# A selective-scan layer with router: turned input products as diagonal products on TensorE, and the state sum in [channel, time]

## The chip, the cores and the metric

The kernel runs on one core of a Trainium2 chip. The metric is the device time of one execution in microseconds. The engines are PE (TensorE: matrix products and transposes), DVE (VectorE), ACT (ScalarE), POOL (GpSimd) and SP (SyncE, which issues the DMAs). In the profile a matrix instruction has two rows, PE for the stream and PEld for the loading of its stationary operand.

## The reference, cut to what matters

Two sequences of 2048 positions with 512 features go through a state-space layer and then a layer that weighs 64 expert biases. All is float32. The part that the change touches is the scan:

```python
delta = jax.nn.softplus(x @ W_delta_1 @ W_delta_2 + b_delta_2)     # [b, l, 1024]
Bm = x @ W_B; Cm = x @ W_C                                          # [b, l, 16]
def step(h, inp):                                                   # h: [b, e = 1024, n = 16]
    A_bar = jnp.exp(d_l[:, :, None] * A)
    h = h * A_bar + (d_l * x_l)[:, :, None] * B_l[:, None, :]
    y_l = jnp.einsum('ben,bn->be', h, C_l)
    return (h, y_l)
...
y_skip = (y + x * W_D) * _silu(skip)
return resid + y_skip @ W_out
```

For each channel e and state n the kernel needs u = (delta x)[e, l] B[l, n], the recurrence along l, and the sum over n of h[e, l] C[l, n].

## The kernel before, in words

The 4096 positions are cut into 16 chunks of 256. Every engine's program is written out by hand as a loop over steps, and within a step over 32 slots. In step t the scan works on chunk t - 3; two chunks form a stage of 512 positions, and a step scans a half of the 1024 channels over the whole stage, in two quarters (256 channels, held as two tiles `q` of 128). One slot is one state n of one quarter: 16 states times 2 quarters are 32 slots. Other jobs ride along in fixed slots: `norm` three chunks ahead, `prep` (in-projection, convolution, delta, B and C) two ahead, `gate` one behind, `mix` (skip product, gate, output product) two behind, `route` (router and experts) three behind. So steps 0 and 1 of the scan have no mix, the last two have no prep, and three steps stand before the scan and three behind it.

One slot runs like this. ACT makes the decay exp(delta A) (`decay`, L703), a 128x512 tile for each q. For 6 of the 16 states (`PLAIN_STATES`) the decay goes into the PSUM tile `bank[:, q]` and POOL makes u with a 128x1024 product into `operand` (`make_u`, L592), from a row of B that a DMA spread over all partitions. For the other 10 the decay goes into `operand`; u is made turned, in [time, channel], where B is a number per partition: ACT multiplies the turned dx (`dx_t`) by it (`make_ut`, L722), and PE turns it back, 4 transposes of 128x128 for each q, into `bank[:, q]` (`turn_u`, L1129). DVE then scans each q (L953) and copies the last column to `carry` (L924). POOL multiplies h by C (`weigh`, L608), and PE adds the result over the 16 states in the PSUM tile `y_sum`, which lies as [time, channel]: 8 transposing 128x128 instructions a slot that accumulate (`add_y`, `add_turned`, L1134), behind 8 products of x with diag(D) at the first state of a quarter (L1152).

There is one `bank` for each q: the transposes of slot s + 1 wait for the scan of slot s in the same q, and the scan of slot s + 1 waits for them. Each engine takes its instructions strictly in the order written. PE's order within slot s is: u of slot s + 1 for q = 0, half of the sum for slot s - 2, side work, u for q = 1, the other half of the sum, side work. DVE's is the two scans of slot s, then its side work: convolution (L1013), x (L993), expert sum o (L1103), and the gate (L1037) and its product (L1049).

`mix` reads the sum back from DRAM as `acc` in [time, channel], PE turns it into `mixed` (L1329), and DVE multiplies it with the gate into `ys`. The output product (L1339) then takes `ys` as its stationary operand.

```python
for b in range(SB):
    last = transpose(bank[:, q, b * P:(b + 1) * P], u_t[:, j % 2, b, q * P:(q + 1) * P], ident[:])
```

Of the kernel before, what the change touches and what calls it, by code (L numbers as in the profile page):

```python
# [23 lines left out]
N = 16  # L24
# [21 lines left out]
NORMED = 8  # L46

# [52 lines left out]
PLAIN_STATES = (0, 3, 5, 8, 11, 13)  # L100
TURNED_STATES = tuple(n for n in range(N) if n not in PLAIN_STATES)


def turned_u(n):

    return n in TURNED_STATES


def before(states, s):

    return s // N * len(states) + sum(n < s % N for n in states)


def build(nc, resid, norm_w, w_skip, w_in, conv_w, conv_b, w_delta_1, w_delta_2, b_delta_2, w_b, w_c, a_log,
# [13 lines left out]
    y_dram = nc.dram_tensor("y_dram", [2, 2, PAIRS, P, TB, QE], F32).ap()  # L128
# [5 lines left out]
    with ExitStack() as stack:  # L134
# [35 lines left out]
        y_out = sb("y_out", P, SB, QE)  # L170


        acc = sb("acc", P, 2, TB, QE)
        thg, gate = sb("thg", P, 2, 2, T), sb("gate", P, 2, 2, T)
# [13 lines left out]
        y_sum = stack.enter_context(nc.psum_tensor("y_sum", [P, SB, QE], F32))  # L188
# [14 lines left out]
        u_ready = signal("u_ready", "scan", before(PLAIN_STATES, SLOTS))  # L203
        ut_ready = signal("ut_ready", "scan", before(TURNED_STATES, SLOTS))
        ut_turned = signal("ut_turned", "scan", 2 * before(TURNED_STATES, SLOTS))
# [8 lines left out]
        b_loaded = [loads_of(f"b_loaded{k}", "scan", before(PLAIN_STATES, SLOTS) // 2) for k in range(2)]  # L214
# [25 lines left out]
        y_turned, ys_ready = signal("y_turned", "mix", PAIRS), signal("ys_ready", "mix", PAIRS)  # L240
# [105 lines left out]

        def prepared(t, half):

            return (FIRST + t) // 2 * 2 + half - 2 - FIRST
# [5 lines left out]
        with nc.Block() as block:  # L355
            @block.sync
            def _(sp):
                def load_quarter(t, k):
# [11 lines left out]
                    if v := due(sp, u_ready, t - 1, len(PLAIN_STATES) * (k + 1)):  # L370
                        sp.wait_ge(u_ready.sem, v)
# [15 lines left out]
                def load_b(t, s):  # L387
# [5 lines left out]
                    if turned_u(n):  # L393
                        return
                    j = before(PLAIN_STATES, s)
# [40 lines left out]
                def load_acc(t, p):  # L436
# [6 lines left out]
                    if v := due(sp, y_turned, t, p - 1):  # L443
                        sp.wait_ge(y_turned.sem, v)
                    sp.dma_start(acc[:, p % 2], y_dram[chunk // 2 % 2, chunk % 2, p]).then_inc(
                        acc_loaded[p % 2].sem, 16)

                def store_y(t, k):
# [9 lines left out]
                    sp.dma_start(y_dram[stage % 2, :, quarter].rearrange("h p b e -> p h b e"),  # L458
                                 y_out[:].rearrange("p (h b) e -> p h b e", h=2)).then_inc(y_stored.sem, 16)
# [101 lines left out]
            def _(pool):  # L561
# [15 lines left out]
                def make_u(t, s):  # L577
# [4 lines left out]
                    _, _, n, k, number = place(t, s)  # L582
                    if turned_u(n):
                        return
                    j = before(PLAIN_STATES, s)
# [96 lines left out]
            def _(act):  # L682
# [3 lines left out]
                def decay(t, s, q):  # L686
# [7 lines left out]
                    if turned_u(n):  # L694
# [11 lines left out]
                def make_ut(t, s, pair):  # L706
# [4 lines left out]
                    stage, _, n, k, _ = place(t, s)  # L711
                    if not turned_u(n):
                        return
                    j = before(TURNED_STATES, s)
                    if v := due(act, dxt_ready, t, 2 * k + pair + 1):
                        act.wait_ge(dxt_ready.sem, v)
                    if v := due(act, bt_ready, prepared(t, pair), 1):
                        act.wait_ge(bt_ready.sem, v)
                    if v := due(act, ut_turned, t, 2 * j - 2):
                        act.wait_ge(ut_turned.sem, v)  # L720
                    for b in (2 * pair, 2 * pair + 1):
                        last = nc.scalar.activation(u_t[:, j % 2, b], dx_t[:, k, b], ACT.Copy,  # L722
                                                    scale=b_t[:, stage % 2, b, n:n + 1])
                    if pair:
                        last.then_inc(ut_ready.sem, 1)

                def take_dxt(t, k, pair):
                    if not slot_of(t, 0):
                        return
                    if v := due(act, dxt_turned, t, 2 * k + pair + 1):  # L730
# [4 lines left out]
                def take_y(t, k):  # L735
# [6 lines left out]
                    for pair in range(2):  # L742
# [639 lines left out]
```

## Time and profile before

| what | value |
|---|---|
| device time, median of 3 runs | 2380.34 us (2379.85 to 2382.69) |
| the profiled execution's own time | 2379.91 us |
| its span in the profile | 2378.0 us |
| busy share: PE, DVE, ACT, POOL | 82%, 75%, 70%, 80% |
| mean granted TensorE clock | 0.939 of full |
| first scan, last scan start | 124.9 us, 2221.6 us |

The profiled execution has 1.9 us outside its span, and lies 0.4 us under the median. The span falls into a head of 124.9 us before the first scan, 16 steps of 32 slots up to the start of the last scan, and a tail of 156.4 us. Busy shares are unions of rows; a PE row is longer than the distance to the next one, since matrix instructions overlap. So what a PE instruction costs in a dense stretch is read from the distance between starts.

### The profile page before, as it was taken

Reading aid. Unit: us, or ns where it says so; the run is one execution under the profiler, and the core shown is the slowest. Engines: PE = TensorE matmul, PEld = TensorE weight load, DVE = VectorE, ACT = ScalarE, POOL = GpSimd, SP = SyncE. Lnnn points to the kernel's source line nnn. Section 1 sums busy time; section 2 is a strip of 40 time slices with the busy share of each in tenths; the row PEclk is TensorE's granted clock in tenths of the full one; section 3 lists DMA queues with packets and bytes.
Section 4 is the critical chain, followed back from the end, with each engine's and each line's share of the span. In section 5 each row is a group of like instructions: output and inputs, shape, how many; then the busy total and the mean of one; then the engine's idle time right before and its main releaser. Section 6 shows DMA issues by size and latency. Waiting matters only on the chain. (4 is left out here: it accounts for less than half of the span.)

```text
span 2378.0 us, 35550 instructions
## 1 busy us (share of the span) xinstructions
PE 1958.7 (82%) x11717; PEld 1584.2 (67%) x11717; DVE 1795.4 (75%) x3105; ACT 1669.1 (70%) x3276; POOL 1913.5 (80%) x1192
## 2 busy tenths in 40 slices
PE   5577777898889898898889898898889988797883
PEld 3456666777667676777667686776667776666551
DVE  3377877798697977888697977889697887887522
ACT  2368686877769685787779686786868687787421
POOL 1279898898789797989879897998879898999512
PEclk9988988999999999999999999999999999999996
DMA  4555556665747565674657556574757646555320
GB/s 159 169 178 182 189 177 215 201 216 157 225 151 239 180 215 183 203 229 150 210 175 235 196 186 215 185 228 148 232 169 222 194 154 207 181 183 160 120 71 18
DMA packets 239281, 434.31 MB, mean 183 GB/s; under 512 B 19134, under 2 KB 135418, under 8 KB 239098
## 3 DMA queue, kind: packets, MB, share of 16 engines
q1 hardware_dynamic: 239098, 432.04, 56.9%
q8 instruction: 94, 1.54, 0.3%
q14 instruction: 89, 0.73, 0.1%
HBM read 347.57 MB, written 84.41 MB: 182 GB/s over the span
## 5 line engine op out<-in xcount | busy, mean ns | idle before, releaser
L608 POOL TENSOR_TENSOR hc<-h,c_all 128x1024 f32<-128x1024 f32 x512 | 1205.0, 2365 | 219.5 <-DVE h L953 160.0
L953 DVE TENSOR_TENSOR_SCAN h<-operand,carry,bank 128x512 f32<-128x512 f32 x480 | 597.1, 1271 | 174.1 <-PE bank L1129 142.7
L1134 PE MATMUL y_sum<-ident,hc 128*128 128x128 f32 x4096 | 624.7, 281 | 13.0 <-POOL hc L608 12.7
L1129 PE MATMUL bank<-ident,u_t 128*128 128x128 f32 x2560 | 417.3, 288 | 243.2 <-DVE h L953 219.7
L722 ACT ACTIVATE u_t<-dx_t,b_t 128x256 f32<-128x256 f32 x1280 | 575.0, 499 | 0.5 <-PE bank L1129 0.5
L1129 PEld LDWEIGHTS bank<-ident,u_t 128*128 128x128 f32 x2560 | 312.4, 148 | 375.1 <-issue 240.2
L1134 PEld LDWEIGHTS y_sum<-ident,hc 128*128 128x128 f32 x4096 | 506.1, 146 | 79.8 <-issue 50.2
L592 POOL TENSOR_TENSOR operand<-dx_q,b_all 128x1024 f32<-128x1024 f32 x192 | 454.5, 2367 | 11.0 <-DMA b_all<-bc_dram 11.0
L703 ACT ACTIVATE bank<-delta_q,neg_a 128x512 f32<-128x512 f32 x384 | 262.5, 684 | 263.1 <-DVE h L953 262.7
L703 ACT ACTIVATE operand<-delta_q,neg_a 128x512 f32<-128x512 f32 x640 | 432.9, 714 | 0.0
L953 DVE TENSOR_TENSOR_SCAN h<-bank,carry,operand 128x512 f32<-128x512 f32 x288 | 354.9, 1270 | 33.1 <-POOL operand L592 16.4
L1339 PE MATMUL mixed<-wout,ys 128*128 128x512 f32 x512 | 272.8, 623 | 3.5 <-DVE ys L1049 3.5
L1259 PE MATMUL pair_bank<-rnt,win 128*128 128x256 f32 x1024 | 261.9, 404 | 11.1 <-DVE x L993 9.0
L1315 PE MATMUL routed<-rnt_gate,wskip 128*128 128x256 f32 x1024 | 245.2, 384 | 22.9 <-DVE gate L1037 18.9
L953 DVE TENSOR_TENSOR_SCAN h<-operand,bank 128x512 f32<-128x512 f32 x160 | 189.7, 1211 | 66.4 <-PE bank L1129 48.4
L1259 PEld LDWEIGHTS pair_bank<-rnt,win 128*128 128x128 f32 x1024 | 201.6, 205 | 57.1 <-issue 28.5
L1315 PEld LDWEIGHTS routed<-rnt_gate,wskip 128*128 128x128 f32 x1024 | 187.2, 191 | 54.6 <-issue 29.6
L1013 DVE SCALAR_TENSOR_TENSOR hv<-pair_bank,taps,hv 128x253 f32<-128x253 f32 (+2 forms) x384 | 181.5, 473 | 0.0
L953 DVE TENSOR_TENSOR_SCAN h<-bank,operand 128x512 f32<-128x512 f32 x96 | 112.8, 1210 | 46.9 <-ACT bank L703 36.5
L684 ACT ACTIVATE hv<-pair_bank,cbias,taps 128x253 f32<-128x253 f32 x128 | 64.9, 557 | 103.9 <-PE pair_bank L1259 103.9
L642 POOL TENSOR_TENSOR dx<-delta,x 128x1024 f32<-128x1024 f32 x32 | 75.6, 2365 | 34.5 <-ACT delta L815 34.5
L1339 PEld LDWEIGHTS mixed<-wout,ys 128*128 128x128 f32 x512 | 81.9, 197 | 29.1 <-issue 22.4
(124 smaller groups left out, 2009.3 us busy)
## 6 DMA issues: line engine op xcount, KB each, us to landing
c_all<-bc_dram SPq DMA_DIRECT2D x256, 512.0 KB, 4.3
b_all<-bc_dram SPq DMA_DIRECT2D x192, 256.0 KB, 5.2
win<-in_L_attn_W_in SPq DMA_DIRECT2D x64, 512.0 KB, 5.7
wskip<-in_L_attn_W_skip SPq DMA_DIRECT2D x64, 512.0 KB, 6.2
x_dram<-x SPq DMA_DIRECT2D x64, 256.0 KB, 4.5
delta_dram<-delta SPq DMA_DIRECT2D x32, 512.0 KB, 7.3
dx_dram<-dx SPq DMA_DIRECT2D x32, 512.0 KB, 7.3
delta_q<-delta_dram SPq DMA_DIRECT2D x32, 512.0 KB, 5.8
```

The costliest lines, as they stand in the source:

```text
L592: nc.gpsimd.tensor_tensor(operand[:, number % 3], dx_q[:, k], b_all[:, j % 2:j % 2 + 1].to_broadcast([P, 2, SPAN]), ALU.mult).then_inc(u_r ...
L608: nc.gpsimd.tensor_tensor(hc[:, number % 3], h[:, number % 3], c_all[:, j % 2, s % 2:s % 2 + 1].to_broadcast([P, 2, SPAN]), ALU.mult).then ...
L642: nc.gpsimd.tensor_tensor(dx[:, part], delta[:, part], x[:, part], ALU.mult).then_inc(dx_ready.sem, 1)
L703: nc.scalar.activation(to, delta_q[:, k, q], ACT.Exp, scale=neg_a[:, et, n:n + 1]).then_inc(exp_ready.sem, 1)
L722: last = nc.scalar.activation(u_t[:, j % 2, b], dx_t[:, k, b], ACT.Copy, scale=b_t[:, stage % 2, b, n:n + 1])
L953: nc.vector.tensor_tensor_scan(h[:, number % 3, q], first, second, start, ALU.mult, ALU.add).then_inc(scan_done.sem, 1)
L1013: return nc.vector.scalar_tensor_tensor(out=to, in0=of, scalar=taps[:, et, k:k + 1], in1=onto, op0=ALU.mult, op1=ALU.add)
L1129: last = transpose(bank[:, q, b * P:(b + 1) * P], u_t[:, j % 2, b, q * P:(q + 1) * P], ident[:])
L1134: return matmul(to, lhsT=of, rhs=ident[:], is_transpose=True, start=start, stop=stop, skip_group_check=True)
L1259: last = matmul(pair_bank(p)[:, e * T:(e + 1) * T], win[:, p % 2, k, e * P:(e + 1) * P], rnt[:, k, :], start=(k == 0), stop=(k == KD - 1))
L1315: last = matmul(routed[:, e * T:(e + 1) * T], wskip[:, p % 2, k, e * P:(e + 1) * P], rnt_gate[:, k, :], start=(k == 0), stop=(k == KD - 1))
L1339: last = matmul(mixed[:], ys[:, et, b * P:(b + 1) * P], wout[:, et, :], start=(et == 0), stop=(et == ET - 1))
```

## The change

It has five parts. (1) u of 24 slots in 32 instead of 20 is made on PE, and POOL keeps 8 instead of 12. (2) On PE those are no longer transposes of ACT's product, but products: the stationary operand is the turned dx, and the moving one is diag(B), a 128x128 tile for each block of 128 positions. ACT now makes diag(B) from the identity (128x128) instead of u (128x256), into a ring of 4. (3) `y_sum` lies as [channel, time]: h C is added by a product with the identity, one 128x512 instruction for each q. (4) `mix` therefore reads `acc` as it needs it; PE's turning of it is gone, the gate stays in the PSUM tile `routed`, and DVE multiplies that with `acc`. (5) The in-projection of the first channel pair of a chunk stands one slot earlier, and the second half of the output product one slot later.

```diff
-PLAIN_STATES = (0, 3, 5, 8, 11, 13)
+PLAIN_SLOTS = (0, 4, 7, 10, 16, 21, 27, 30)
...
-    y_dram = nc.dram_tensor("y_dram", [2, 2, PAIRS, P, TB, QE], F32).ap()
+    y_dram = nc.dram_tensor("y_dram", [2, PAIRS, P, 2, SPAN], F32).ap()
...
-        u_t = sb("u_t", P, 2, SB, QE)
+        diag_b = sb("diag_b", P, RING, SB, P)
...
-                def make_ut(t, s, pair):
+                def make_diag(t, s, pair):
...
-                    if v := due(act, ut_turned, t, 2 * j - 2):
-                        act.wait_ge(ut_turned.sem, v)
+                    if v := due(act, u_turned, t, 2 * (j - RING + 1)):
+                        act.wait_ge(u_turned.sem, v)
+                    ring = ring_of(t, j)
                     for b in (2 * pair, 2 * pair + 1):
-                        last = nc.scalar.activation(u_t[:, j % 2, b], dx_t[:, k, b], ACT.Copy,
+                        last = nc.scalar.activation(diag_b[:, ring, b], ident[:], ACT.Copy,
                                                     scale=b_t[:, stage % 2, b, n:n + 1])
...
                                         nc.vector.scalar_tensor_tensor(
-                                            out=gate[:, p % 2].rearrange("p e t -> p (e t)"),
-                                            in0=thg[:, p % 2].rearrange("p e t -> p (e t)"), scalar=1.0,
+                                            out=routed[:], in0=thg[:, p % 2].rearrange("p e t -> p (e t)"), scalar=1.0,
...
                                         nc.vector.tensor_tensor(
-                                            ys[:, 2 * p:2 * p + 2, :].rearrange("p e t -> p (e t)"), mixed[:],
-                                            gate[:, p % 2].rearrange("p e t -> p (e t)"),
+                                            ys[:, 2 * p:2 * p + 2, :].rearrange("p e t -> p (e t)"), routed[:],
+                                            acc[:, p % 2].rearrange("p e t -> p (e t)"),
                                             ALU.mult).then_inc(ys_ready.sem, 1)
...
                     for b in range(SB):
-                        last = transpose(bank[:, q, b * P:(b + 1) * P], u_t[:, j % 2, b, q * P:(q + 1) * P],
-                                         ident[:])
-                    last.then_inc(ut_turned.sem, 1)
+                        last = matmul(bank[:, q, b * P:(b + 1) * P], dx_t[:, k, b, q * P:(q + 1) * P],
+                                      diag_b[:, ring_of(t, j), b], start=True, stop=True)
+                    last.then_inc(u_turned.sem, 1)
...
-                        for b in (2 * pair, 2 * pair + 1):
-                            for q in range(2):
-                                last = matmul(y_sum[:, b, q * P:(q + 1) * P], lhsT=x_q[:, q, b * P:(b + 1) * P],
-                                              rhs=diag_d[:, 2 * quarter + q], start=b % 2 == 0 and q == 0,
-                                              stop=False, skip_group_check=True)
+                        last = matmul(y_sum[:, q], lhsT=diag_d[:, 2 * quarter + q], rhs=x_q[:, q], start=True,
+                                      stop=False)
...
-                    for b in (2 * pair, 2 * pair + 1):
-                        for q in range(2):
-                            last = add_turned(y_sum[:, b, q * P:(q + 1) * P], hc[:, number % 3, q, b * P:(b + 1) * P],
-                                              False, n == N - 1)
+                    last = matmul(y_sum[:, q], lhsT=ident[:], rhs=hc[:, number % 3, q], start=False, stop=n == N - 1)
...
-                                if (s, late) in ((3 * p - 2, 1), (3 * p - 1, 0)):
+                                first = 3 * p - 2 if p else -3
+                                if (s, late) in ((first, 1), (first + 1, 0)):
...
-                                if s == 3 * p + 15 and not late:
...
-                                            last = transpose(mixed[:, (2 * e + b) * P:(2 * e + b + 1) * P],
-                                                             acc[:, p % 2, b, e * P:(e + 1) * P], ident[:])
```

The first place is PE in the middle of a step that has a mix job, around slots 14 to 16: u into `bank`, the sum into `y_sum`, the skip product into `routed`. Before:

```order
L1129 MATMUL bank<-ident,u_t 128x128 x4
L1134 MATMUL y_sum<-ident,hc 128x128 x4
L1277 MATMUL pair_bank<-x,wbc 32x256 x4
L1315 MATMUL routed<-rnt_gate,wskip 128x256 x4
L1134 MATMUL y_sum<-ident,hc 128x128 x4
L1329 MATMUL mixed<-ident,acc 128x128 x4
L1134 MATMUL y_sum<-ident,hc 128x128 x4
```

The same place after the change:

```order
L1130 MATMUL bank<-diag_b,dx_t 128x128 x4
L1153 MATMUL y_sum<-hc,ident 128x512
L1269 MATMUL pair_bank<-x,wbc 32x256 x4
L1307 MATMUL routed<-rnt_gate,wskip 128x256 x4
L1153 MATMUL y_sum<-hc,ident 128x512 x2
```

Four transposing instructions of 128 columns have become one product of 512 columns, the four transposes into `bank` four products, and the turning of `acc` is gone.

The second place is PE at the end of a step, slots 29 to 31, with the first in-projection of the next chunk (`win`). Before:

```order
L1184 MATMUL pair_bank<-ident,dx_q 128x128 x4
L1129 MATMUL bank<-ident,u_t 128x128 x4
L1134 MATMUL y_sum<-ident,hc 128x128 x4
L1129 MATMUL bank<-ident,u_t 128x128 x4
L1134 MATMUL y_sum<-ident,hc 128x128 x4
L1259 MATMUL pair_bank<-rnt,win 128x256 x4
L1134 MATMUL y_sum<-ident,hc 128x128 x4
L1259 MATMUL pair_bank<-rnt,win 128x256 x4
```

After:

```order
L1175 MATMUL pair_bank<-ident,dx_q 128x128 x4
L1251 MATMUL pair_bank<-rnt,win 128x256 x4
L1130 MATMUL bank<-diag_b,dx_t 128x128 x4
L1153 MATMUL y_sum<-hc,ident 128x512
L1251 MATMUL pair_bank<-rnt,win 128x256 x4
L1130 MATMUL bank<-diag_b,dx_t 128x128 x4
L1153 MATMUL y_sum<-hc,ident 128x512 x3
```

The in-projection now stands right behind the turning of dx, and not behind the sum of the next slots.

## Rows read from the trace of the kernel before

**Rows 1.** The page: busy time, share of the span and instructions of each engine.

```profile
PE 1958.7 (82%) x11717; PEld 1584.2 (67%) x11717; DVE 1795.4 (75%) x3105; ACT 1669.1 (70%) x3276; POOL 1913.5 (80%) x1192
```

**Rows 2.** Stretches: head, scan span, tail, and two neighbouring full steps.

```profile
core 0: us, PE busy (x) PEld busy (x) DVE busy (x) ACT busy (x) POOL busy (x), PEclk, DMA share, GB/s
0.00:124.90 124.90, 71.66 (x274) 53.62 (x275) 41.87 (x133) 42.84 (x90) 22.29 (x46) 0.90 0.53 175
124.90:2221.60 2096.70, 1784.86 (x11055) 1466.42 (x11055) 1710.31 (x2860) 1594.95 (x3127) 1855.87 (x1086) 0.95 0.60 192
2221.60:2378.00 156.40, 102.13 (x392) 64.15 (x390) 43.20 (x113) 31.31 (x60) 35.32 (x61) 0.84 0.18 61
...
1452.90:1584.90 132.00, 117.16 (x734) 95.62 (x733) 112.64 (x194) 103.89 (x205) 117.35 (x74) 0.97 0.63 201
1584.90:1726.00 141.10, 120.41 (x734) 97.44 (x733) 112.65 (x194) 104.07 (x205) 121.67 (x76) 0.95 0.62 193
```

**Rows 3.** Groups by line and form on PE, whole span.

```profile
L1134 PE MATMUL y_sum<-ident,hc 128*128 128x128 f32 x4096 | 624.7, 281 | 13.0 <-POOL hc L608 12.7
...
L1129 PE MATMUL bank<-ident,u_t 128*128 128x128 f32 x2560 | 417.3, 288 | 243.2 <-DVE h L953 219.7 <-ACT u_t L722 19.4
...
L1339 PE MATMUL mixed<-wout,ys 128*128 128x512 f32 x512 | 272.8, 623 | 3.5 <-DVE ys L1049 3.5
...
L1152 PE MATMUL y_sum<-diag_d,x_q 128*128 128x128 f32 x512 | 67.7, 275 | 0.7 <-ACT y_out L744 0.7
...
L1152 PEld LDWEIGHTS y_sum<-diag_d,x_q 128*128 128x128 f32 x512 | 65.8, 192 | 4.4 <-issue 2.1
```

**Rows 4.** PE's timeline in slots 0 to 2: start, time, line.

```profile
1460.62 0.60 PE L1134 MATMUL y_sum<-ident,hc 128*128 128x128 f32 x4
1461.06 1.02 PE L1339 MATMUL mixed<-wout,ys 128*128 128x512 f32 x2
1461.92 0.60 PE L1134 MATMUL y_sum<-ident,hc 128*128 128x128 f32 x4
...
1464.58 1.89 PE L1259 MATMUL pair_bank<-rnt,win 128*128 128x256 f32 x8
1466.31 1.05 PE L1152 MATMUL y_sum<-diag_d,x_q 128*128 128x128 f32 x8
1467.19 0.60 PE L1134 MATMUL y_sum<-ident,hc 128*128 128x128 f32 x4
```

**Rows 5.** Waits on PE and DVE, 1183.4 to 1726 us (four steps): total, times, longest.

```profile
PE bank L1129 <- DVE h L953: 48.3, 30, 5.2
PE pair_bank L1184 <- DMA dx_q<-dx_dram: 12.0, 2, 6.3
...
DVE h L953 <- PE bank L1129: 48.0, 33, 9.2
```

**Rows 6.** DVE's timeline behind the scans of slots 3 and 6.

```profile
1471.23 0.13 DVE L924 TENSOR_REDUCE carry<-h 128x2 f32<-128x2 f32 x1
1471.28 0.68 DVE L993 SCALAR_TENSOR_TENSOR x<-pair_bank,hv 128x512 f32<-128x512 f32 x1
...
1473.94 2.44 DVE L953 TENSOR_TENSOR_SCAN h<-operand,carry,bank 128x512 f32<-128x512 f32 x2
...
1484.68 0.13 DVE L924 TENSOR_REDUCE carry<-h 128x2 f32<-128x2 f32 x1
...
1488.05 2.44 DVE L953 TENSOR_TENSOR_SCAN h<-operand,carry,bank 128x512 f32<-128x512 f32 x2
```

**Rows 7.** Groups on ACT and POOL that the change touches, whole span.

```profile
L722 ACT ACTIVATE u_t<-dx_t,b_t 128x256 f32<-128x256 f32 x1280 | 575.0, 499 | 0.5 <-PE bank L1129 0.5
...
L592 POOL TENSOR_TENSOR operand<-dx_q,b_all 128x1024 f32<-128x1024 f32 x192 | 454.5, 2367 | 11.0 <-DMA b_all<-bc_dram 11.0
...
L748 ACT ACTIVATE diag_d<-ident,dskip 128x128 f32<-128x128 f32 x8 | 2.4, 387 | 0.7 <-PEq L322 0.7
```

More of the change, by code:

```diff
@@ L46 @@
 NORMED = 8
+RING = 4
 class Signal:
@@ L97, in jobs_of, with turned_u, before @@
     return tuple(job for job, chunk in ahead.items() if 0 <= chunk < CHUNKS)
-PLAIN_STATES = (0, 3, 5, 8, 11, 13)
[L101 to L111, printed above, removed]
+PLAIN_SLOTS = (0, 4, 7, 10, 16, 21, 27, 30)
+TURNED_SLOTS = tuple(s for s in range(SLOTS) if s not in PLAIN_SLOTS)
+def turned_u(s):
+    return s in TURNED_SLOTS
+def before(slots, s):
+    return s // SLOTS * len(slots) + sum(n < s % SLOTS for n in slots)
 def build(nc, resid, norm_w, w_skip, w_in, conv_w, conv_b, w_delta_1, w_delta_2, b_delta_2, w_b, w_c, a_log,
@@ L213, in build @@
         xq_loaded, y_stored = loads_of("xq_loaded", "scan", 2), loads_of("y_stored", "scan", 2)
-        b_loaded = [loads_of(f"b_loaded{k}", "scan", before(PLAIN_STATES, SLOTS) // 2) for k in range(2)]
+        b_loaded = [loads_of(f"b_loaded{k}", "scan", before(PLAIN_SLOTS, SLOTS) // 2) for k in range(2)]
         c_loaded = [loads_of(f"c_loaded{k}", "scan", SLOTS // 4) for k in range(2)]
@@ L581, in make_u @@
                     t, s = now
-                    _, _, n, k, number = place(t, s)
-                    if turned_u(n):
+                    _, _, _, k, number = place(t, s)
+                    if turned_u(s):
                         return
-                    j = before(PLAIN_STATES, s)
+                    j = before(PLAIN_SLOTS, s)
                     if v := due(pool, scan_done, t, 2 * (s - 2)):
@@ L741, in take_y @@
                         act.wait_ge(y_stored.sem, v)
-                    for pair in range(2):
-                        part = slice(2 * pair, 2 * pair + 2)
-                        nc.scalar.activation(y_out[:, part], y_sum[:, part], ACT.Copy,
-                                             scale=0.5).then_inc(y_read.sem, 1)
+                    for q in range(2):
+                        nc.scalar.activation(y_out[:, q], y_sum[:, q], ACT.Copy, scale=0.5).then_inc(y_read.sem, 1)
                 for et in range(ET):
@@ L939, in scan @@
                         dve.wait_ge(carry_saved.sem, v)
-                    if not turned_u(n):
-                        if v := due(dve, u_ready, t, before(PLAIN_STATES, s) + 1):
+                    if not turned_u(s):
+                        if v := due(dve, u_ready, t, before(PLAIN_SLOTS, s) + 1):
                             dve.wait_ge(u_ready.sem, v)
@@ L1120, in turn_u @@
                     t, s = now
-                    if not turned_u(place(t, s)[2]):
+                    if not turned_u(s):
                         return
-                    j = before(TURNED_STATES, s)
-                    if v := due(pe, ut_ready, t, j + 1):
-                        pe.wait_ge(ut_ready.sem, v)
+                    k, j = s // N, before(TURNED_SLOTS, s)
+                    if v := due(pe, diag_ready, t, j + 1):
+                        pe.wait_ge(diag_ready.sem, v)
+                    if v := due(pe, dxt_ready, t, 2 * k + 2):
+                        pe.wait_ge(dxt_ready.sem, v)
                     if v := due(pe, scan_done, t, 2 * (s - 1) + q + 1):
@@ L1143, in add_y @@
                     if n == 0:
-                        if t == -FIRST and k == 0 and pair == 0:
+                        if t == -FIRST and k == 0 and q == 0:
                             pe.wait_ge(diag_made, ET)
@@ L1174, in turn_dx @@
                     if k:
-                        for read, step in ((gate_ready, t - 1), (o_ready, t - 1)):
+                        for read, step in ((ys_ready, t - 1), (o_ready, t - 1)):
                             if v := due(pe, read, step, read.per):
```

106 lines of the change are left out of this document (46 added, 60 removed).

## The prediction, made before the changed kernel was run

> **What bounds the kernel now.** I read the page first: four engines are busy for 70% to 82% of the span, and none is at its limit [rows 1]. The stretches say the same of a full step: in 132.0 and 141.1 us PE is busy 117 to 120, POOL 117 to 122, DVE 113, ACT 104 [rows 2]. So no single engine sets the pace; the chains between them do. The waits name the main one: over four steps PE stood 48.3 us before u of a slot because DVE had not finished the last scan in that `bank`, and DVE stood 48.0 us before a scan because PE had not filled `bank` [rows 5]. The two hand one buffer to and fro, and side work on either side delays the other.
>
> For this change what counts is how much work PE has in a step. Busy time can't tell that, as its rows overlap, so I take distances between starts in a dense stretch [rows 4]: four transposing instructions of 128 columns take 0.44 us (1460.62 to 1461.06), or 0.11 each. The group L1339 is one instruction of 512 columns in the program and shows as two records; they take 0.86 us (1461.06 to 1461.92). Eight records of 256 columns take 1.73 us, 0.216 each. Eight records of L1152, which are four 128x128 products with diag(D), take 0.88 us, so 0.22 for one product. A float32 product is two records where a transpose is one: L1339 has 512 records for its 16 x 16 instructions, L1134 has 4096 for 16 x 32 x 8 [rows 3]. **A product of 128 columns thus costs 0.22 us, a transpose 0.11.**
>
> PE's need in a full step before: 256 transposing adds 28.2, 160 transposes of u 17.6, 32 records of diag(D) 3.5, 16 for `acc` 1.8, sum 51.1 us. The rest: 176 records of 256 columns (in, skip, both delta products, B and C) 38.0, 16 output products 13.8, 2 expert products of 512 columns 1.7, 32 other transposes 3.5, 20 router records 2.2, sum 59.2. Together 110 of about 136 us; the rest is waiting, and stretches at the lower clock (the granted clock is 0.95 to 0.97 in full steps, [rows 2]).
>
> **What each part costs.**
> The sum in [channel, time]: 64 products of 512 columns at 0.86 = 55.0 us a step, for 28.2. It moves the same columns, but with arithmetic.
> u on PE: 24 slots x 8 = 192 products of 128 columns at 0.222 = 42.6 us, for 17.6. Of L1152, the nearest row, the load of the stationary operand reads 192 ns and the products still come 0.11 us apart [rows 3, 4], so loads are hidden; new in u is only that every product has its own stationary tile, and L1152 has that too.
> diag(D): 4 products of 512 columns, 3.4 us for 3.5. The turning of `acc`: 1.8 us less.
> Sum on PE: 101.0 us for 51.1, **49.9 us a step more**, and a full step needs 160.2 us of PE. That is above the 132 to 141 us that a step takes now, so PE becomes the bound whatever else gets faster.
> POOL: 4 products of 2.367 us a step less [rows 7], 9.5 us. It is no longer waited for, so this is worth nothing; without PE's new load it could not have been worth more than these 9.5 us a step.
> ACT: 80 activations at 575.0/1280 = 0.449 us (35.9) become 96 of 128x128, by L748 between 0.30 (its union) and 0.387 us (its mean): 29 to 37 us, a change of -7 to +1, under PE's cover, as ACT is busy 104 us. Were the cover gone it would cost at most that 1 us.
> DVE: the gate and its product are the same two instructions with other operands; 0.
> The DMAs: 4 loads of B a step less, y moved in as many bytes; 0, as only PE's wait for dx_q shows among the waits (12.0 us in four steps, [rows 5]). A slot gets longer from about 4.2 to 5.2 us, and PE comes to that place later against the loads, so I take this wait as gone.
> The earlier in-projection: no cost on PE, since both places lie in a stretch full of PE work. It frees ACT and DVE at slot 0, where they are not the bound any more: 0. The output product a slot later: 0, the same work.
>
> **The sum.** Between the first and the last scan PE needs: 16 steps x (101.0 + 1.8 for turning dx) = 1645; 14 preps x 24.2 = 339; 13 norms x 0.9 = 12; 14 mixes x 27.6 less the 6.9 that fall behind the last scan = 379; 13 routes x 4.8 less some 3 = 60. That is 2435 us.
> To it comes what PE still waits for. PE and DVE stay tied through `bank`. In a row of turned slots PE has 3.5 us and DVE 2.4 us of its own, and PE never waits. At a plain slot it can: take PE's end of u for slot 3 as zero. DVE scans for 1.3 us, then does x and the convolution for 2.7 (1471.23 to 1473.94), and scans q = 0 of slot 4: 5.3 us until PE may write u of slot 5. PE meanwhile has half a sum and an output product (1.7), the sum of slot 3's turn (1.7) and another 1.1: 4.5. It waits 0.8. At slot 6 DVE has 3.4 us of side work (1484.68 to 1488.05) [rows 6]: 5.9 against 5.4, a wait of 0.5. At slot 9: 5.3 against 3.0, a wait of 2.3. In the second half of a step PE's side work is heavier and DVE's lighter, and the same count gives under 0.5 a plain slot. In all some 6 to 7 us in a full step; 11 in each of the first two, where PE has no output product under the convolutions; about 2 in the last two. Over 16 steps: 12 x 6.5 + 22 + 4 = 104.
> Head 124.9 and tail 156.4 stay: the head has no scan, and the tail loses only transposes of `acc`. Span: 124.9 + 2435 + 104 + 156.4 = 2820; with the 1.9 us around it 2822, and against the median 0.4 more. I say **2825 us**, 18.7% slower.
>
> **A rule set against the rows.** A transpose runs at 0.11 us per 128 columns and a float32 product at 0.22, twice as much [rows 4]. The Trainium skill (TensorE: Matmul & The Clock Gate, Terms) gives the transpose mode as 4 times faster for float32. By it a product of 128 columns would cost 0.44 us here, and the sum, with four times a transpose for all that the change turns into products, would come out near 4470 us. The rows show twice, and I take them.
>
> **The rivals.**
> *The gaps stay.* PE's need rises as above, but it goes on waiting as now. Now the scan span of 2096.7 us holds some 1640 us of need by the same count, 455 unfilled. If the waits on DVE (48.3 us in four steps, [rows 5]) and some 6 us of cold clock and issue gaps remain, 18 a step: 124.9 + 2435 + 288 + 156.4 = 3004. For it speaks that the chain through `bank` is untouched; against it that DVE's own time, 113 us, fits nearly one and a half times into 160. Chance 0.15.
> *The products cost no more than transposes* (the other side). An operand that is the identity or a diagonal might stream in one record. PE's need would be 59.2 + 28.2 + 21.1 + 1.8 = 110 us, POOL falls from 117 to 108, and the step could fall by up to the 9.5 us of POOL: 2380 - 150 = 2230. L1152, with diag(D), speaks against it: two records for each product. It decides where a product of 128 columns costs under about 0.15 us: the step has some 26 us to fill and the change adds 50 at 0.22, so at 0.11 + 0.11 x 26/50 = 0.167 the step is full, and some of it must stay for waits. Chance 0.03.
> *Four times a transpose.* A load of the stationary operand that isn't hidden, or passes that the operands here need and L1152 doesn't: 0.44 a product of 128 columns gives 64 x 1.76 + 192 x 0.44 + 7 = 204 us for 101, a step of 263, and 2825 + 16 x 103 = 4470 us. L1339 at 512 columns in 0.86 us speaks against it. Chance 0.02. (This is how the page's rule above would show.)
> *Forecast:* PE is the bound and mostly full. Chance 0.80.
>
> **How the numbers follow.** The floor is no wait at all: 124.9 + 2435 + 156.4 + 2 = 2718; the pitch rounding (0.109 read as 0.11, over a step's 250 records) moves it by 15 either way. The forecast's own range is 2760 to 2920 (a wait of 3 to 12 us a step). To hold 8 in 10 I take in the lower part of the rival of the gaps: 2755 to 2950. Slower by over 0.2%, about what a measurement of this kernel can tell from no change: 0.96; faster 0.03; within 0.01.
>
> **What the profile after should show.** PE busy over 93% of the span, granted clock at or near 1.0 in all inner slices; y_sum 2048 records of 512 columns, 0.86 us a pair; bank 6144 records, 0.22 a pair; a full step of 163 to 170 us; POOL busy near 1760, DVE unchanged at 1795; DVE's and ACT's waits now on PE (bank), over 500 us for DVE; PE's waits for DVE under 120 us, most at slots 9 and 10. The prediction is wrong if a full step is under 155 or over 180 us, or if records of L1130 come closer than 0.10 or wider than 0.13 us apart.

## The result, and the profile after

The changed kernel takes 2856.6 us in the median of 4 runs (2853.52 to 2859.76), against 2380.1 us before (4 runs): 1.200 times as long, 95% interval 1.198 to 1.202. The forecast was 2825 us, with a range of 2755 to 2950.

The page of the changed kernel: busy time of each engine, the granted clock in 40 slices, the chain that ended last by engine, and two groups of PE and one of ACT.

```profile
PE 2672.5 (94%) x12613; PEld 1830.4 (64%) x12613; DVE 1814.1 (64%) x3105; ACT 1615.5 (57%) x3532; POOL 1771.8 (62%) x1128
...
PEclk9899999999999999999999999999999999999986
...
PE 73%; DVE 4%; issue 1%; POOL 1%; ACT 0%; DMA 0%; POOLq 0%; DVEq 0%; SPq 0%
...
L1153 PE MATMUL y_sum<-hc,ident 128*128 128x512 f32 x2048 | 1027.8, 597 | 0.0
...
L1130 PE MATMUL bank<-diag_b,dx_t 128*128 128x128 f32 x6144 | 825.1, 278 | 65.3 <-DVE h L956 64.8
...
L725 ACT ACTIVATE diag_b<-ident,b_t 128x128 f32<-128x128 f32 x1536 | 524.5, 391 | 0.0
```

PE went from 82% to 94% of the span while every other engine's share fell [rows 1]. The sum is now 2048 records of 512 columns, two for each of 1024 instructions. The idle time before u because of DVE fell from 219.7 us [rows 3] to 64.8. POOL's busy time fell by 142 us. Before, PE had waited 12.7 us for it [rows 3] and DVE 24.9 us (first line below, kernel before); in the changed kernel neither a sum nor a scan waits for it. DVE's waits for PE grew from 191.1 us to 756.8 (second line, changed kernel):

```profile
DVE h L953 <- POOL operand L592: 24.9, 19, 3.0
...
DVE h L956 <- PE bank L1130: 756.8, 526, 4.9
```

The stretches of the changed kernel (length, busy time of PE, PEld, DVE, ACT, POOL, granted clock, DMA share, GB/s): head, scan span, tail, two neighbouring full steps.

```profile
0.00:124.70 124.70, 71.55 (x277) 53.61 (x278) 41.88 (x134) 42.60 (x90) 22.22 (x46) 0.90 0.53 170
124.70:2681.60 2556.90, 2489.52 (x11989) 1711.05 (x11988) 1728.52 (x2859) 1541.68 (x3383) 1715.07 (x1022) 0.99 0.47 151
2681.60:2851.70 170.10, 111.46 (x350) 65.71 (x348) 43.67 (x113) 31.17 (x60) 34.49 (x60) 0.80 0.17 56
1409.70:1576.80 167.10, 163.72 (x789) 112.77 (x788) 110.14 (x196) 100.73 (x221) 110.77 (x71) 1.00 0.48 155
1576.80:1743.90 167.10, 163.71 (x789) 112.76 (x788) 110.10 (x196) 100.64 (x221) 110.73 (x71) 1.00 0.47 155
```

A full step takes 167.1 us and PE is busy for 163.7 of it. Before, odd and even steps differed (132.0 and 141.1 us), though PE's work in them hardly did (117.2 and 120.4 us busy); now they are equal, and PE is busy for 98% of each. The granted clock is at its upper level (2.4 GHz) throughout a full step. Of the 473.7 us by which the span grew, the scan span has 460, the tail 14 (156.4 to 170.1), the head nothing [rows 2].

PE's timeline of the changed kernel behind slots 6 and 9: start, time, line, and in brackets the idle time.

```profile
1449.37 1.02 PE L1319 MATMUL mixed<-wout,ys 128*128 128x512 f32 x2
1451.48 1.13 PE L1130 MATMUL bank<-diag_b,dx_t 128*128 128x128 f32 x8 [1.09 <-DVE h L956]
1452.45 1.02 PE L1153 MATMUL y_sum<-hc,ident 128*128 128x512 f32 x2
1453.31 1.05 PE L1130 MATMUL bank<-diag_b,dx_t 128*128 128x128 f32 x8
1454.20 1.02 PE L1153 MATMUL y_sum<-hc,ident 128*128 128x512 f32 x2
1455.15 1.12 PE L1222 MATMUL routed<-ebias,low 64*128 64x512 f32 x2
...
1465.84 0.60 PE L1175 MATMUL routed<-ident,dx_q 128*128 128x128 f32 x4
1468.73 1.13 PE L1130 MATMUL bank<-diag_b,dx_t 128*128 128x128 f32 x8 [2.29 <-DVE h L956]
```

One product of 512 columns takes 0.86 us (1452.45 to 1453.31) and four of 128 columns 0.89 us (1453.31 to 1454.20), as L1339 and L1152 did before [rows 4]. Over the two steps shown in the stretches PE's only waits are these for DVE:

```profile
PE bank L1130 <- DVE h L956: 6.8, 4, 2.3
```

That is 3.4 us a step in two waits, 1.1 us at slot 6 and 2.3 us at slot 9.

### The profile page after: what moved, and what is told of

Read it like the earlier page. It is cut to its first block, busy times and chain, and to the rows that moved or that the text cites. A ratio compares the mean times of both kernels' runs of the same rounds, so it can differ in the third digit from the quotient of the medians.

```text
span 2851.7 us, 37433 instructions
## 1 busy us (share of the span) xinstructions
PE 2672.5 (94%) x12613; PEld 1830.4 (64%) x12613; DVE 1814.1 (64%) x3105; ACT 1615.5 (57%) x3532; POOL 1771.8 (62%) x1128
## 4 chain that ended last, share of the span: by engine, by line
PE 73%; DVE 4%; issue 1%; POOL 1%; ACT 0%; DMA 0%; POOLq 0%; DVEq 0%; SPq 0%
PE y_sum L1153 23%; PE bank L1130 20%; PE routed L1307 7%; PE mixed L1319 7%; PE pair_bank L1251 5%; PE y_sum L1147 2%; PE pair_bank L1269 1%; PE pair_bank L1261 1%; PE pair_bank L1289 1%; PE routed L1222 1%; DVE hv L1016 1%; PE routed L1206 1%; DVE h L956 1%; PE routed L1197 1%; DVE x L996 1%
## 5 line engine op out<-in xcount | busy, mean ns | idle before, releaser
L956 DVE TENSOR_TENSOR_SCAN h<-operand,carry,bank 128x512 f32<-128x512 f32 x576 | 729.5, 1276 | 578.0 <-PE bank L1130 570.2
L1153 PE MATMUL y_sum<-hc,ident 128*128 128x512 f32 x2048 | 1027.8, 597 | 0.0
L1130 PEld LDWEIGHTS bank<-diag_b,dx_t 128*128 128x128 f32 x6144 | 800.3, 193 | 302.2 <-issue 258.7
L1130 PE MATMUL bank<-diag_b,dx_t 128*128 128x128 f32 x6144 | 825.1, 278 | 65.3 <-DVE h L956 64.8
L707 ACT ACTIVATE operand<-delta_q,neg_a 128x512 f32<-128x512 f32 x768 | 529.7, 712 | 0.0
L725 ACT ACTIVATE diag_b<-ident,b_t 128x128 f32<-128x128 f32 x1536 | 524.5, 391 | 0.0
L1153 PEld LDWEIGHTS y_sum<-hc,ident 128*128 128x128 f32 x2048 | 339.5, 192 | 151.3 <-issue 148.6
L707 ACT ACTIVATE bank<-delta_q,neg_a 128x512 f32<-128x512 f32 x256 | 175.8, 687 | 340.1 <-DVE h L956 339.9
L596 POOL TENSOR_TENSOR operand<-dx_q,b_all 128x1024 f32<-128x1024 f32 x128 | 301.3, 2354 | 11.0 <-DMA b_all<-bc_dram 11.0
L956 DVE TENSOR_TENSOR_SCAN h<-bank,carry,operand 128x512 f32<-128x512 f32 x192 | 235.6, 1268 | 3.8
```

The costliest lines, as they stand in the source:

```text
L596: nc.gpsimd.tensor_tensor(operand[:, number % 3], dx_q[:, k], b_all[:, j % 2:j % 2 + 1].to_broadcast([P, 2, SPAN]), ALU.mult).then_inc(u_r ...
L707: nc.scalar.activation(to, delta_q[:, k, q], ACT.Exp, scale=neg_a[:, et, n:n + 1]).then_inc(exp_ready.sem, 1)
L725: last = nc.scalar.activation(diag_b[:, ring, b], ident[:], ACT.Copy, scale=b_t[:, stage % 2, b, n:n + 1])
L956: nc.vector.tensor_tensor_scan(h[:, number % 3, q], first, second, start, ALU.mult, ALU.add).then_inc(scan_done.sem, 1)
L1130: last = matmul(bank[:, q, b * P:(b + 1) * P], dx_t[:, k, b, q * P:(q + 1) * P], diag_b[:, ring_of(t, j), b], start=True, stop=True)
L1153: last = matmul(y_sum[:, q], lhsT=ident[:], rhs=hc[:, number % 3, q], start=False, stop=n == N - 1)
```

## The experiments

The edits are given against the kernel before or after, whichever the heading names. Every ratio is taken against the kernel before on the run's own chip. Where the medians of two runs on different chips are set against each other, a difference of up to 3 or 4 us says nothing: the kernel before took 2378.0 to 2381.6 us on these chips.

### One part at a time on the kernel before

Four parts were made alone: the sum (with what `mix` needs for it, and with the second half of the output product a slot later), the product for u, the split of slots, and the earlier in-projection.

**The sum in [channel, time] alone.**

```diff
-                            last = add_turned(y_sum[:, b, q * P:(q + 1) * P], hc[:, number % 3, q, b * P:(b + 1) * P],
-                                              False, n == N - 1)
+                    last = matmul(y_sum[:, q], lhsT=ident[:], rhs=hc[:, number % 3, q], start=False, stop=n == N - 1)
```

> The kernel before with only the sum in [channel, time] (parts 3 and 4). Theory A (the time is PE's need, at the distances between starts, plus a few us of waits): PE needs 27 us a step more for the sum and 2 less for acc, 25 in all, so some 139 us in a full step where 136 is taken now; with the waits still there in part, 143 to 150 a step, 2490 to 2600 us. Theory B (what counts is the chain through bank; the sum is off it): 2380 to 2410 us.

Measured: 2518.6 us, ratio 1.059 (1.056 to 1.062), in theory A's range.

**u as a product alone**, with the old 20 slots.

```diff
-                        last = transpose(bank[:, q, b * P:(b + 1) * P], u_t[:, j % 2, b, q * P:(q + 1) * P],
-                                         ident[:])
+                        last = matmul(bank[:, q, b * P:(b + 1) * P], dx_t[:, k, b, q * P:(q + 1) * P],
+                                      diag_b[:, ring_of(t, j), b], start=True, stop=True)
```

> The kernel before with u as a product of turned dx and diag(B), with the old 20 slots. Theory A: PE needs 160 x 0.112 = 18 us a step more, about 132 in all, still under the step of now: 2430 to 2490 us, less than the sum costs. Theory B: every turned slot has 0.45 us more for each q on the chain through bank, 18 us a step, all of it on the path: about 2670 us, much more than the sum costs.

Measured: 2501.9 us, ratio 1.051 (1.049 to 1.053).

Theory B is out: the sum, off the chain through `bank`, costs 138 us, and the product for u, on it, costs 121 and not 290. But e2 came out 12 us above theory A's range, and for fewer microseconds of PE it costs nearly as much. The waits of PE, whole span, first the kernel with the sum alone and then the one with u alone:

```profile
PE bank L1127 <- DVE h L955: 77.0, 38, 3.9
```

```profile
PE bank L1137 <- DVE h L959: 145.6, 79, 4.6
```

Before it was 219.7 us [rows 3]. PE's extra work first fills its waits. The sum, off the chain, adds 25 us a step and leaves 77.0 us of these waits, the product for u, on it, adds 18 and leaves 145.6. Since the two amounts differ, this does not show how much is owed to the place on the chain. DVE became late in both alike: its waits for `bank` are 323.7 us with the sum alone and 322.2 with u alone, for 191.1 before. How the remainder of e2 splits was not taken apart.

**The split of slots alone**: 24 of 32 turned, by transposes as before.

```diff
-PLAIN_STATES = (0, 3, 5, 8, 11, 13)
+PLAIN_SLOTS = (0, 4, 7, 10, 16, 21, 27, 30)
```

> The kernel before with 24 slots in 32 turned, by transposes as before. GpSimd loses 9.5 us a step, PE gains 3.5 and ScalarE 7. Theory A: PE has room, no engine was the bound, so little moves: 2340 to 2390 us. Rival, GpSimd was what held the step: down by up to 150, 2230 to 2300 us.

Measured: 2432.4 us, ratio 1.022 (1.020 to 1.024), slower than either theory had it. GpSimd's busy time fell to 1769.3 us from 1913.5 [rows 1], and the kernel got slower: taking work from that engine does not by itself shorten the step. Here the places of its slots changed as well as their count; the section on the places below takes this miss apart.

**The earlier in-projection alone.**

```diff
-                                if (s, late) in ((3 * p - 2, 1), (3 * p - 1, 0)):
+                                first = 3 * p - 2 if p else -3
+                                if (s, late) in ((first, 1), (first + 1, 0)):
```

> The kernel before with only the first in-projection of a chunk a slot sooner. Slot 0 takes 7.5 us on average and ScalarE waited 103.9 us in all for in-projections. If that wait is what makes slot 0 long, it falls by 2 to 3 us a step: 2335 to 2350 us. If it only makes room for the next wait: 2370 to 2385 us.

Measured: 2386.1 us, ratio 1.0023 (1.0013 to 1.0034). That is 1 us above the range of the second outcome and nothing like the first: no gain. In the trace of this kernel the wait for the in-projection fell and others took its place:

```profile
DVE h L958 <- PE bank L1134: 224.6, 167, 9.6
...
ACT hv L689 <- PE pair_bank L1265: 80.9, 43, 5.5
```

Before, the second line stood at 103.9 us and the first at 191.1 us. Its scan span is 2094.8 us long for 2096.7 before [rows 2], its head 129.2 for 124.9; why the head of some kernels is 2 to 4 us longer stays open.

**Slots and in-projection together**, still with transposes only.

> The kernel before with 24 slots turned by transposes and the first in-projection sooner, without any product in place of a transpose. If neither is on the path: 2370 to 2390 us. If slot 0 and GpSimd both gave waits: 2290 to 2350 us, faster than both kernels.

Measured: 2433.2 us, ratio 1.021 (1.019 to 1.023), as with the slots alone, and outside both outcomes.

Alone, the sum, u, the slots and the in-projection cost 138, 121, 51 and 5 us, 315 together; the change costs 476. Of the difference, some 57 us are the four slots more whose transposes are products in the change and not in e3 (32 x 0.112 x 16, an estimate). The other 100 or so were not taken apart. They fit with idle time of PE that each part alone still finds to fill, and that all together can fill only once.

### The price of a product in the changed kernel

```diff
-                    for b in range(SB):
+                    for b in (*range(SB), *range(SB)):
                         last = matmul(bank[:, q, b * P:(b + 1) * P], dx_t[:, k, b, q * P:(q + 1) * P],
```

> The changed kernel with every product for u issued twice into the same place (the same result). Theory A, PE is the bound: 16 x 192 more products at 0.222 us, 682 us, so about 3540 us, 3500 to 3560. If PE were not the bound, or waits took up part of it: under 3400.

Measured: 3543.5 us, ratio 1.488 (1.484 to 1.491). 3072 products more cost 686.9 us, **0.2236 us for one of 128 columns**. The group of u in this kernel, with the idle time before it:

```profile
L1130 PE MATMUL bank<-diag_b,dx_t 128*128 128x128 f32 x12288 | 1519.2, 277 | 63.5 <-DVE h L956 63.1
```

The waits before u are as long as in the changed kernel (64.8 us), so all that is added to PE's queue is added to the time. The added products lie on the chain through `bank`, so their full price alone would also fit a kernel in which that chain sets the pace. What speaks against it is that PE would then wait for DVE in every turned slot; it waits 63.5 us in 3541, and no longer than with half the products: PE is full.

### Work given back to GpSimd

```diff
-PLAIN_SLOTS = (0, 4, 7, 10, 16, 21, 27, 30)
+PLAIN_SLOTS = (0, 3, 5, 8, 11, 13, 16, 19, 21, 24, 27, 29)
```

> The changed kernel with the old split of slots: 12 in 32 back on GpSimd instead of 8. Theory A: PE needs 32 x 0.222 = 7.1 us a step less and GpSimd has room (111 of 167 us busy), so it gets faster by 16 x 7.1 = 114 us, to some 2743 us (2730 to 2775). Rival, that GpSimd's relief was worth something in the changed kernel: 2857 us or more.

Measured: 2733.8 us, ratio 1.148 (1.145 to 1.151), in the range of theory A. 512 products less, at 0.2236 us, are 114.5 us of the 122.8 gained, and PE's waits for DVE fell by 14 us (64.8 to 50.5). This edit also moves the places of GpSimd's slots, though, and e12 below shows that places alone are worth 59 us in this kernel. With e12's eight places kept, which are among the twelve of this table, giving back the other four gains 63 us (2797.2 to 2733.8). So the offload to PE is itself a loss in the changed kernel: it takes work from an engine with room and puts it on the one without. The scan span of this kernel, and its waits for DVE:

```profile
128.40:2566.80 2438.40, 2381.07 (x10968) 1605.03 (x10967) 1723.12 (x2860) 1472.80 (x3127) 1859.27 (x1086) 0.99 0.52 165
```

```profile
PE bank L1130 <- DVE h L956: 50.5, 33, 2.7
```

### The tail: when the skip product may start

In the tail no scan covers the chain skip product, tanh, gate, product with `acc`. PE's timeline there, first before, then of the changed kernel.

```profile
2252.66 3.69 PE L1315 MATMUL routed<-rnt_gate,wskip 128*128 128x256 f32 x16 [1.06 <-DVE gate L1037]
2256.18 0.60 PE L1329 MATMUL mixed<-ident,acc 128*128 128x128 f32 x4
2257.85 3.69 PE L1315 MATMUL routed<-rnt_gate,wskip 128*128 128x256 f32 x16 [1.06 <-DVE gate L1037]
```

```profile
2709.08 6.12 PE L1307 MATMUL routed<-rnt_gate,wskip 128*128 128x256 f32 x16 [3.97 <-DVE ys L1048]
2717.50 5.33 PE L1307 MATMUL routed<-rnt_gate,wskip 128*128 128x256 f32 x16 [2.30 <-DVE ys L1048]
2725.14 3.69 PE L1307 MATMUL routed<-rnt_gate,wskip 128*128 128x256 f32 x16 [2.30 <-DVE ys L1048]
```

As the gate now stays in `routed`, the next skip product has to wait for `ys` too. The turning of `acc`, which filled 0.4 us of that wait, is gone, and two of the three blocks shown take 5.3 and 6.1 us for 3.7 (of the eight blocks in the tail, four are so long, and one was before); the granted clock of the tail is 0.80 for 0.84 before [rows 2]. Two kernels let the skip product wait for the gate alone.

**The gate in an SBUF tile of its own.**

```diff
-                                            out=routed[:], in0=thg[:, p % 2].rearrange("p e t -> p (e t)"), scalar=1.0,
+                                            out=gate[:, p % 2].rearrange("p e t -> p (e t)"), in0=thg[:, p % 2].rearrange("p e t -> p (e t)"), scalar=1.0,
...
-                                    if v := due(pe, ys_ready, t, p):
-                                        pe.wait_ge(ys_ready.sem, v)
+                                    if v := due(pe, gate_ready, t, p):
+                                        pe.wait_ge(gate_ready.sem, v)
```

> The changed kernel with the gate in a tile of its own again, so that the next skip product waits for the gate and not for its product with acc. Theory: the tail, 13.7 us longer than before, has six waits of 2.3 to 4.0 us for ys where it had six of 1.1 to 2.7 us for the gate, and records at the lower clock behind them; it gets 8 to 10 us shorter, and the steps stay the same: 2846 to 2850 us. Rival, the tail is longer for PE's backlog at the last scan: no change.

Measured: 2887.4 us, ratio 1.213 (1.210 to 1.215), 31 us slower and not 8 faster. The tail did what the theory said, the scan span did not: its stretches, and the product with `acc`.

```profile
125.00:2723.30 2598.30, 2507.53 (x11992) 1719.10 (x11991) 1802.34 (x2859) 1540.34 (x3383) 1721.29 (x1022) 0.99 0.47 149
2723.30:2885.40 162.10, 105.75 (x350) 61.99 (x348) 46.62 (x113) 31.16 (x60) 35.14 (x60) 0.83 0.18 59
```

```profile
L1050 DVE TENSOR_TENSOR ys<-gate,acc 128x512 f32<-128x512 f32 x64 | 123.1, 1923 | 6.7
```

The tail is 162.1 us for 170.1. The scan span is 41 us longer, and the product takes 1.92 us. In the changed kernel it is 0.69:

```profile
L1048 DVE TENSOR_TENSOR ys<-routed,acc 128x512 f32<-128x512 f32 x64 | 44.3, 692 | 6.7
```

Both its operands now lie in SBUF, and GpSimd is at work.

**The gate in the PSUM tile `mixed`**, so that the product has one operand in PSUM.

```diff
-                                            out=routed[:], in0=thg[:, p % 2].rearrange("p e t -> p (e t)"), scalar=1.0,
+                                            out=mixed[:], in0=thg[:, p % 2].rearrange("p e t -> p (e t)"), scalar=1.0,
```

> The changed kernel with the gate written to the PSUM tile mixed, which is free then: the next skip product waits for the gate alone, as in e7, but the product with acc has one operand in PSUM, as in the changed kernel. If e7 lost its time because that product read two SBUF tiles while GpSimd worked (1.92 us in the mean for 0.69): the tail falls by 8 us to about 162, the steps stay at 167.4, 2846 to 2851 us. If e7 lost it through the earlier release of the skip products: about 2885 again.

Measured: 2844.3 us, ratio 1.196 (1.193 to 1.199), 2 us under the first outcome. Its scan span, tail, and the same product:

```profile
127.30:2683.50 2556.20, 2488.63 (x11992) 1711.31 (x11991) 1728.58 (x2860) 1541.69 (x3383) 1714.86 (x1022) 0.99 0.47 151
2683.50:2846.30 162.80, 107.04 (x350) 62.58 (x348) 43.75 (x113) 31.18 (x60) 34.49 (x60) 0.82 0.18 58
```

```profile
L1052 DVE TENSOR_TENSOR ys<-mixed,acc 128x512 f32<-128x512 f32 x64 | 44.3, 692 | 6.7
```

The product is back at 0.69 us, the scan span at 2556 us, and the tail is 7 us shorter. So e7's loss was the two SBUF operands, and the tail's growth is for over half the longer wait of the skip product. Against the changed kernel the intervals of the whole just touch (1.193 to 1.199 against 1.198 to 1.202); the traces show the part in the tail.

### Where GpSimd's slots lie

**24 slots turned by transposes, on the kernel before, with GpSimd's 8 at states where they lay before.**

```diff
-PLAIN_STATES = (0, 3, 5, 8, 11, 13)
+PLAIN_SLOTS = (0, 3, 8, 13, 16, 19, 24, 29)
```

> The kernel before with 24 slots in 32 turned by transposes, as in e3, but GpSimd's 8 slots lie at states where they lay before (0, 3, 8, 13 of each quarter). If e3 was slower because of where the slots lie: 2365 to 2395 us. If it is the count (3.5 us more on PE, 7 on ScalarE, and four more slots that pass the bank to and fro): 2415 to 2445, as e3.

Measured: 2348.6 us, ratio 0.988 (0.985 to 0.991), **faster than both kernels**, by 1.2% than the kernel before, and 16 us under the better outcome that I had named. The same counts in other places take 84 us less than e3 (80 by the two ratios). Two steps of e3, then two of e9:

```profile
1066.70:1348.80 282.10, 247.73 (x1529) 203.47 (x1528) 223.26 (x389) 220.31 (x441) 220.97 (x141) 0.95 0.58 183
```

```profile
1052.00:1319.00 267.00, 239.83 (x1530) 196.21 (x1528) 222.26 (x390) 220.38 (x441) 221.34 (x140) 0.99 0.61 194
```

All engines have the same instructions, but PE is busy 8 us longer in e3, at a granted clock of 0.95 for 0.99, and its waits for DVE in the whole span are 259.7 us for 199.7. So the places cost waits, and the waits go with a lower clock. Which of the moved slots does it was not tried apart. Nor is it known what makes this kernel faster than the one before: GpSimd has less work in it, and its slots lie elsewhere.

**14 slots on GpSimd**, 7 of each quarter.

> The kernel before with 14 slots in 32 on GpSimd instead of 12, 7 of each quarter. GpSimd's need rises by 4.7 us to about 121 of 136 a step, PE's falls by 1.8. If the count of turned slots is what costs: 2350 to 2375 us, faster than both kernels. If GpSimd is near its limit, or the balance of before was already the best: 2385 to 2430.

Measured: 2402.9 us, ratio 1.009 (1.006 to 1.013). That lies in the second outcome. But here too the places had to differ, so this run tells only that this table isn't better, and nothing of the count of turned slots.

**The changed kernel with the places of e9.**

```diff
-PLAIN_SLOTS = (0, 4, 7, 10, 16, 21, 27, 30)
+PLAIN_SLOTS = (0, 3, 8, 13, 16, 19, 24, 29)
```

> The changed kernel with the places of GpSimd's 8 slots from e9, which alone were worth 84 us between e3 and e9. Theory A, PE is full and places only shift which slot waits: within 15 us of the changed kernel, 2842 to 2872. If the places are worth the same here: about 2775.

Measured: 2797.2 us, ratio 1.175 (1.172 to 1.178), 59 us faster than the changed kernel: between what I had expected and the other outcome. The stretch of its scan span, and its waits for DVE in the whole span:

```profile
125.20:2622.80 2497.60, 2474.26 (x11992) 1704.83 (x11991) 1727.46 (x2859) 1539.97 (x3383) 1715.45 (x1022) 1.00 0.49 155
```

```profile
PE bank L1130 <- DVE h L956: 20.8, 27, 2.7
```

The waits fell from 64.8 to 20.8 us, and PE's busy time in the scan span by 15 us (2489.5 to 2474.3). 44 + 15 is the 59 us. Most of the 15 is the clock (granted 0.99 in the changed kernel, 1.00 here): the clock records of the two traces have the lower level (1.2 GHz) for some 40 us of the scan span there and 16 here, and what is done in 24 us at half the clock takes 12 us less at the full one (an estimate). My expectation was wrong because it forgot that a full engine still had 65 us of waits to lose. With them nearly gone this kernel stands close to what PE's work takes: 2474 us busy in a scan span of 2498.

## Why the prediction was right

**PE becomes the bound.** Right. Every step of the argument that names a bound held: PE busy 94% (said: over 93%), a full step of 167.1 us (said: 163 to 170), and the price of further PE work in e5 is its full length.

**A product costs twice a transpose.** Right, and the ground of the forecast: 0.22 us was read from L1152 before, 0.2236 is the price in e5. The rule of four times a transpose is refuted here, as is the rival by which a product costs no more than a transpose.

**PE's need.** Mis-sized: 2435 us between first and last scan. Busy time there is 2489.5 us (rows in a dense stretch join up), and in e12, nearly without waits, 2474; so the term was 40 to 55 us, about 2%, too low. A full step has 163.7 us for my 160.2. From start to start in the step of 1409.7 us, u takes 43.3 us (said 42.6), the sum 55.5 (55.0), the output products 14.2 (13.8), the 256-column records 38.3 (38.0), the expert products 2.1 (1.7), the router's records 2.9 (2.2) and the other transposes 3.9 (3.5). Each term is a little low. Records at a change of line stand a little further apart than in a dense stretch: the product for the sum and the next one are not always 0.86 us apart, as 1454.20 to 1455.15 shows (0.95) before L1222. The 15 us that I allowed for rounding did not cover it, and do not follow from their own working: 0.001 us on 250 records of 16 steps is 4 us.

**What PE still waits for.** Mis-sized the other way: 104 us forecast, 67 measured between the first and last scan (2556.9 less 2489.5 busy). The places were right for two of three: 0.5 us was foreseen at slot 6 and 1.1 measured, 2.3 at slot 9 and 2.3 measured; the 0.8 at slot 3 didn't show, and the profile was to have most of the waits at slots 9 and 10 where it has them at 6 and 9. The three us a step foreseen beyond these were not there. The first two steps came as forecast (282.4 us with 263.3 busy: 19 idle, for 22), the last two had none (for 4); the miss lies in the twelve full steps, 48 us for 78. In the sum, PE's need came out 54 us too low by its busy time, the waits 37 too high and the tail 14 too low, which makes the 32 us between 2825 and 2856.6. That the sum was closer than its largest error is luck.

**Head and tail stay.** The head did. The tail grew by 13.7 us, where I had counted only what the change removes. The step that failed is "the tail loses only transposes": part (4) also puts `routed` in use until `ys` is done, and I had costed the gate and its product as "the same two instructions", without naming who waits behind them. e7 and e11 show 7 to 8 us of it; the rest, the sum's longer products behind the last scan among it, was not tried.

**POOL, ACT, the DMAs, the in-projection at nothing.** POOL: right, its relief is worth nothing in the changed kernel, and the work taken from it costs 63 us there at fixed places (e8 against e12). The 104 us of waits had been worked out for the places of its slots in the change; that other places would cost less was not asked, and e12 shows 59 us in them. The in-projection: right on the kernel before (e4, e6); on the changed kernel it was not tried alone, nor was the later output product. DVE: 1814 us for 1795 [rows 1], with no instruction added (3105 in both); what of it is on the path is its part in PE's waits, counted above. ACT's rows of diag(B) have a mean of 391 ns, a union of 524.5/1536 = 341 ns, within the bounds of 0.30 to 0.387 for the cost of one; the 35.9 us a step became 32.8. PE's wait for dx_q is gone from the full steps, as forecast.

**The rivals.** The gaps did not stay (3004 us): here a chain that set the pace while every engine had room stopped doing so once one engine had none. It is not that the chain went away. e2 shows it at half way: 145.6 us of waits for DVE where PE's need is 18 us a step more.

## What to carry to other kernels

Count an engine's need from distances between starts in a dense stretch, and add what a change brings before asking what it relieves: once it is above the length of a step, it sets the time. Here PE's need with head and tail gave 2718 us, 5% under the measured time, and with an estimate of the waits 2825, 1% under. A float32 transpose that becomes a float32 product with the identity or a diagonal matrix moves the same columns at twice the time, and an offload to the engine that this fills is a loss even if the other engine was busy for 80%. Where slots of one engine lie among another's can be worth as much as such a part of a change (84 us before, 59 after), so compare two splits of work at the same places. Where an instruction's output moves to another memory, look at who waits for the old place and at where both operands of the reader lie.

## What the runs showed of the hardware

A DVE product of two 128x512 tiles took 0.69 us with one operand in PSUM (before, after, and e11) and 1.92 us in the mean with both in SBUF beside a working GpSimd (e7); single ones took from 0.692 to 2.854 us. Three of them in e7, with the GpSimd product next to each:

```profile
1534.49 2.35 POOL L612 TENSOR_TENSOR hc<-h,c_all 128x1024 f32<-128x1024 f32 x1 [1.02 <-PE y_sum L1155]
1534.69 2.69 DVE L1050 TENSOR_TENSOR ys<-gate,acc 128x512 f32<-128x512 f32 x1
...
1549.65 2.36 POOL L612 TENSOR_TENSOR hc<-h,c_all 128x1024 f32<-128x1024 f32 x1 [1.27 <-DVE h L956]
1550.32 2.24 DVE L1050 TENSOR_TENSOR ys<-gate,acc 128x512 f32<-128x512 f32 x1
...
1858.00 0.69 DVE L1050 TENSOR_TENSOR ys<-gate,acc 128x512 f32<-128x512 f32 x1
1858.43 2.48 POOL L612 TENSOR_TENSOR hc<-h,c_all 128x1024 f32<-128x1024 f32 x1 [2.70 <-PE y_sum L1155]
```

The first two began after GpSimd's product and ended 0.54 and 0.55 us after it, however much of it was left when they began; the third began first, took 0.69 us, and GpSimd's took 2.48 for 2.35. The Trainium skill (SBUF — State Buffer, section "SBUF: two separate sides") states that an instruction of DVE with two SBUF inputs and one of GpSimd that reads SBUF contend for a port pair, that whichever starts first has it for the whole instruction, and that the other waits. The trace agrees: the longest is 2.16 us over the shortest, within one GpSimd product of 2.36 us.

A slot table with the same counts on every engine moved the time by 84 us of 2400 (e3 against e9). In two steps, 15 us longer in e3, the same PE records were busy 8 us longer, at a granted clock of 0.95 for 0.99. So the waits of these places cost more than their own length: the records ran longer as well, at the lower clock.
